# Cross-attention values as one-pass products of split context sums and split Wv

## What is computed

```python
q = rmsnorm((layernorm(x) @ Wq).reshape(B, Sq, H, D), gq)   # B=16, Sq=100, dim=512, H=16, D=128
k = rmsnorm((ctx @ Wk).reshape(B, Skv, H, D), gk)           # Skv=361, cdim=256
v = (ctx @ Wv).reshape(B, Skv, H, D)
attn = softmax(einsum('bqhd,bkhd->bhqk', q, k) / sqrt(D))
out = einsum('bhqk,bkhd->bqhd', attn, v).reshape(B, Sq, H * D)
x = x + out @ Wo
x = x + ffn(layernorm(x))      # rotations, 8-bit activations, ternary weights
```

## Time and profile before

| | |
|---|---|
| median of three runs | 1384.07 us (1384.0 to 1386.38) |
| the profiled execution | 1386.21 us, span 1384.4 us |
| TensorE products | 1361.0 us busy (98%) |
| VectorE | 949.7 us (69%) |
| ScalarE | 939.1 us (68%) |
| GpSimd | 442.0 us (32%) |
| granted TensorE clock, mean | 1.000 |

### The profile page before, as it was taken

The page is one execution under the profiler, slowest core; times in us unless marked ns, Lnnn a source line. Parts: engine busy times, 40 slices in busy tenths (PEclk is TensorE's granted clock), DMA queues, the critical chain, the costliest instruction groups (busy, mean ns, idle before and its releaser), DMA issues. The chain is left out here.

```text
span 1384.4 us, 28300 instructions
## 1 busy us (share of the span) xinstructions
PE 1361.0 (98%) x9496; PEld 1211.0 (87%) x9496; DVE 949.7 (69%) x2478; ACT 939.1 (68%) x2083; POOL 442.0 (32%) x349
## 2 busy tenths in 40 slices
PE   9999989999999999999999999999999999999997
PEld 9889867999999999999999999998878888888885
DVE  6312047668777877777778777776558778887886
ACT  5556668888888888888888888888734443444342
POOL 1034314322112212211222212213735555565551
PEclk9999999999999999999999999999999999999999
DMA  8867823333444444444434443435462342334212
GB/s 251 232 173 207 236 55 110 104 109 105 138 114 128 120 119 119 138 116 115 138 112 121 129 119 118 121 101 139 146 186 61 82 95 62 69 71 106 62 31 43
DMA packets 186403, 166.36 MB, mean 120 GB/s; under 512 B 87938, under 2 KB 155540, under 8 KB 184468
## 3 DMA queue, kind: packets, MB, share of 16 engines
q1 hardware_dynamic: 178980, 151.50, 39.6%
q10 hardware_dynamic: 7280, 13.06, 3.6%
HBM read 124.57 MB, written 33.02 MB: 114 GB/s over the span
## 5 line engine op out<-in xcount | busy, mean ns | idle before, releaser
L804 POOL TENSOR_TENSOR rk_sp<-ms_sp,neg_half 124x6 f32<-124x6 f32 x128 | 170.7, 1354 | 615.9 <-DMA ms_sp<-ms 615.9
L1028 ACT ACTIVATE pr<-ex,ri 100x361 f32<-100x361 f32 x256 | 153.6, 600 | 68.4 <-DVE ri L1228 68.4
L1240 DVE CUSTOM_DVE_ANT_0 sc<-psS,rk 100x361 f32<-100x361 f32 x256 | 136.3, 532 | 80.7 <-PE psS L879 65.7
L1021 ACT ACTIVATE ex<-sc,nb,rq_all 100x361 f32<-100x361 f32 x256 | 175.9, 687 | 2.2 <-DVE nb L1249 2.1
L907 PE MATMUL psZ<-pT_hi,cK_hi 120*128 120x400 f32 (+1 forms) x384 | 132.7, 346 | 0.0
L907 PE MATMUL psZ<-pT_hi,cK_lo 120*128 120x400 f32 (+1 forms) x384 | 132.2, 344 | 0.0
L907 PE MATMUL psZ<-pT_lo,cK_hi 120*128 120x400 f32 (+1 forms) x384 | 131.9, 344 | 0.0
L892 PEld LDWEIGHTS psP<-ident,pr 100*120 100x120 f32 (+1 forms) x768 | 73.0, 138 | 47.3 <-issue 35.3
L1228 DVE RECIPROCAL ri<-rs 100x1 f32<-100x1 f32 x256 | 41.3, 161 | 91.0 <-ACT ex L1021 87.0
L1220 DVE TENSOR_TENSOR pT_lo<-psP,pT_hi 122x600 fp32r<-122x600 f32 x128 | 99.0, 774 | 1.8 <-ACT pT_hi L1052 1.6
L922 PE MATMUL psNV<-z,wv_sb 128*128 128x200 f32 x504 | 97.2, 336 | 0.8 <-issue 0.8
(11 more groups left out here) (315 smaller groups left out, 3868.6 us busy)
## 6 DMA issues: line engine op xcount, KB each, us to landing
rk<-rk_dram SPq DMA_DIRECT2D x128, 290.6 KB
q_dram<-q_out SPq DMA_DIRECT2D x64, 200.0 KB, 4.6
q_in<-q_dram SPq DMA_DIRECT2D x64, 200.0 KB, 4.0
o_dram<-o SPq DMA_DIRECT2D x64, 200.0 KB, 4.5
stage<-in_w_ff SPq DMA_DIRECT2D x12, 1024.0 KB, 6.5
w_in<-in_w_ff ACTq DMA_DIRECT2D x48, 256.0 KB, 3.7
o_in<-o_dram SPq DMA_DIRECT2D x12, 1024.0 KB, 5.9
cT_in<-in_ctxT SPq DMA_DIRECT2D x15, 361.0 KB, 4.2
```

The source lines that it names most:

```text
L804: nc.gpsimd.tensor_tensor(rk_sp[:, cols], ms_sp[:, cols], neg_half[0:HG * SKR, :].to_broadcast([HG * SKR, n]), op=ALU.pow).then_inc(g_rk, 1)
L1021: nc.scalar.activation(ex[:, h % 2, :], sc[:, h % 2, :], ACT.Exp, bias=nb[:, h % 2:h % 2 + 1], scale=factor(n), accum_out=rs[:, h % 2:h % ...
L1028: nc.scalar.activation(pr[:, h, SKP - SK:SKP], ex[:, h % 2, :], ACT.Copy, scale=ri[:, h % 2:h % 2 + 1]).then_inc(a_pr, 1)
L1240: nc.vector.tensor_tensor_reduce(out=sc[:, h % 2, :], in0=psS[0:SQ, 0:SK], in1=rk[:, u % 2, h, 0:SK], scale=1.0, scalar=-3.0e38, op0=ALU.m ...
```

## The change

The values become three one-pass products per 128-row block: z_hi x wv_hi, z_hi x wv_lo, z_lo x wv_hi, so 12 products instead of 4 float32 ones (8 records) per value.

- Both halves of z are now split: ScalarE writes z_hi (`high_z`, at h=0 and h=2), VectorE z_lo (`low_z`, at h=0 and h=2, behind `negate_max`), both straight from psZ. z has two unit slots instead of four.
- Both values of a pair run in the odd unit: `values(u-3, psNV)` at h=2 and `values(u-2, psZ[1])` at h=3. `copy_o` of the second follows at h=0 of the next unit.
- GpSimd splits the pair's Wv columns (`split_wv`, eight operations of 2x128 columns at h=1 of even units) and the queries (`split_q`, two operations of 400 columns per unit, in place of ScalarE's `high_q` and VectorE's `low_q`). q_in has one slot instead of two, and `load_q` waits for the split of the unit before.
- To make room: seven slots for the squares instead of eight, the exponentials in place of the scores, `below` and `w_out` in one tile that also takes a block of Wo, xn0 and xr0 in w_in.
- One semaphore less in `queries`.

The core of the diff:

```diff
@@ attention: tiles
-        q_in = sb("q_in", [P, 2, UQ])
+        q_in = sb("q_in", [P, UQ])
-        sq = sb("sq2", [P, 2, HG, SKP])
+        sq = sb("sq2", [P, SQS, SKP])
-        ex, pr = sb("ex", [SQ, 2, SK]), sb("pr", [SQ, HG, SKP])
+        pr = sb("pr", [SQ, HG, SKP])
-        z = sb("z", [P, 4, CC, UQ])
+        z_hi, z_lo = sb("z_hi", [P, 2, CC, UQ], F32R), sb("z_lo", [P, 2, CC, UQ], F32R)
+        wv_hi, wv_lo = sb("wv_hi", [P, CC, HG * D], F32R), sb("wv_lo", [P, CC, HG * D], F32R)
@@ SP: load_q
-                if due(held(sp, u - 1)):
-                    sp.wait_ge(v_q, held(sp, u - 1))
+                if due(held(sp, u)):
+                    sp.wait_ge(g_qlo, held(sp, u))
@@ GpSimd
+            def split_q(u):
+                pool.wait_ge(d_q[u % 2], u // 2 * 16 + 16)
+                if due(u * HG - HG):
+                    pool.wait_ge(p_s, u * HG - HG)
+                nc.gpsimd.tensor_copy(q_hi[:, u % 2, :], q_in[:]).then_inc(g_qhi, 1)
+                pool.wait_ge(g_qhi, u + 1)
+                nc.gpsimd.tensor_tensor(q_lo[:, u % 2, :], q_in[:], q_hi[:, u % 2, :].bitcast(F32),
+                                        op=ALU.subtract).then_inc(g_qlo, 1)
+            def split_wv(p):
+                if due(p):
+                    pool.wait_ge(p_v, 2 * p)
+                for h in range(HG):
+                    col = (place(2 * p)[1] * HG + h) * D
+                    part = slice(h * D, (h + 1) * D)
+                    nc.gpsimd.tensor_copy(wv_hi[:, :, part], wv_sb[:, :, col:col + D]).then_inc(g_wv, 1)
+                    pool.wait_ge(g_wv, (p * HG + h) * 2 + 1)
+                    nc.gpsimd.tensor_tensor(wv_lo[:, :, part], wv_sb[:, :, col:col + D], wv_hi[:, :, part].bitcast(F32),
+                                            op=ALU.subtract).then_inc(g_wv, 1)
                     if h == 0 and real(u + 1, UNITS):
                         rms(u + 1, 1)
+                        split_q(u + 1)
+                    if h == 1 and u % 2 == 0 and real(u - 2, UNITS):
+                        split_wv((u - 2) // 2)
@@ TensorE: gather
-                    pe.wait_ge(v_z if c else a_z, u)
+                    pe.wait_ge(v_z, u * CC - CC + 1 + c)
+                if c == 1 and u % 2 == 0 and due(u):
+                    pe.wait_ge(a_o, u)
@@ TensorE: values
-                pe.wait_ge(a_z, first + 2)
-                pe.wait_ge(v_z, first + 2)
-                pe.wait_ge(v_ms, min(v + 6, UNITS))
+                pe.wait_ge(v_z, first * CC + 2 * CC)
+                pe.wait_ge(g_wv, (first // 2 * HG + v % 2 * 2 + 2) * 2)
+                if v % 2 == 0:
+                    pe.wait_ge(v_ms, min(v + 6, UNITS))
...
-                        last = nc.tensor.matmul(bank[:, k * 2 * SQ:(k + 1) * 2 * SQ], wv_sb[:, c, col:col + D],
-                                                z[:, first % 4:first % 4 + 2, c, h * SQ:(h + 1) * SQ],
-                                                start=(c == 0), stop=(c == CC - 1))
+                        for w, x in ((wv_hi, z_hi), (wv_lo, z_hi), (wv_hi, z_lo)):
+                            last = nc.tensor.matmul(bank[:, k * 2 * SQ:(k + 1) * 2 * SQ], w[:, c, h * D:(h + 1) * D],
+                                                    x[:, :, c, h * SQ:(h + 1) * SQ], start=(n == 0), stop=(n == 3 * CC - 1))
+                            n += 1
@@ TensorE: unit
-                    if h == 2 and real(u - 3, UNITS):
+                    if h == 2 and u % 2 == 1 and real(u - 3, UNITS):
                         values(u - 3, psNV)
-                    if h == 2 and u == UNITS + 1:
-                        values(UNITS - 1, psK[1])
                     if h == 3 and real(u - 1, UNITS):
                         gather(u - 1, 0)
+                    if h == 3 and u % 2 == 1 and real(u - 3, UNITS):
+                        values(u - 2, psZ[1])
@@ ScalarE
+            def high_z(u, c):
+                act.wait_ge(p_z, u * CC + 1 + c)
+                if due(u // 2 * 2):
+                    act.wait_ge(p_v, u // 2 * 2)
+                nc.scalar.activation(z_hi[:, u % 2, c, :], psZ[c][:, 0:UQ], ACT.Copy).then_inc(a_z, 1)
@@ VectorE
+            def low_z(u, c):
+                dve.wait_ge(a_z, u * CC + 1 + c)
+                nc.vector.tensor_tensor(z_lo[:, u % 2, c, :], psZ[c][:, 0:UQ], z_hi[:, u % 2, c, :].bitcast(F32),
+                                        ALU.subtract).then_inc(v_z, 1)
@@ VectorE: unit
-                    if h == 2 and real(u - 2, UNITS):
-                        copy_z(u - 2)
...
                         scale_scores(n, u, h)
                         negate_max(n, h)
+                    if h in (0, 2) and real(u - 2, UNITS):
+                        low_z(u - 2, h // 2)
```

More of the change, by code:

```diff
@@ L591, in attention @@
         bound = sb("bound", [P, 2])
-        w_in, below = sb("w_in", [P, 2, DIM]), sb("below", [P, DIM], BF16)
-        w_out = sb("w_out", [P, 2, DIM], FP8)
+        w_in, w_work = sb("w_in", [P, 2, DIM]), sb("w_work", [P, DIM])
+        below = w_work[:, 0:DIM // 2].bitcast(BF16)
+        w_out = w_work[:, DIM // 2:DIM].bitcast(FP8).rearrange("p (a n) -> p a n", a=2)
         psK = [bank0, ctx.enter_context(nc.psum_tensor("psK1", [P, 512], F32))]
@@ L613, in attention @@
                      cK_in[:].rearrange("p i c -> p (i c)")[:, 0:DIM]]
-                    + [sq[:].rearrange("p s h k -> p (s h k)")[:, i * DIM:(i + 1) * DIM] for i in range(5)])
+                    + [sq[:].rearrange("p s k -> p (s k)")[:, i * DIM:(i + 1) * DIM] for i in range(4)] + [w_work[:]])
         WO_HI_AT = {(UNITS - 3, 1): range(0, 4), **{(UNITS - 2, h): (4 + h,) for h in range(HG)}}
@@ L707, in spread_rk @@
                     sp.wait_ge(p_ss, UNITS)
+                    for i in range(2):
+                        sp.wait_ge(d_wt[i], 16 * CHUNKS // 2)
                     for i in range(4, 9):
@@ L866, in squares @@
                     rows = slice(h * QW32, (h + 1) * QW32)
-                    last = nc.tensor.matmul(psNV[rows, 0:SKP], sel[:, QW32 - 1:2 * QW32 - 1], sq[:, u % 2, h, :],
+                    last = nc.tensor.matmul(psNV[rows, 0:SKP], sel[:, QW32 - 1:2 * QW32 - 1], sq[:, (u * HG + h) % SQS, :],
                                             start=True, stop=True, tile_position=(0, h * QW32))
@@ L1097, in unit @@
                         high_cK(u // (2 * NG) * 2 + first - 1)
[L1098 to L1100 removed]
+                    if h == 3 and u % 2 == 1 and real(u - 3, UNITS):
                         copy_o(u - 3, psNV)
[L1102 to L1105 removed]
+                    if h == 0 and u % 2 == 0 and real(u - 3, UNITS):
+                        copy_o(u - 3, psZ[1])
+                    if h in (0, 2) and real(u - 2, UNITS):
+                        high_z(u - 2, h // 2)
                     if real(m, HEADS):
@@ L1287, in unit @@
                         low_cK(u // (2 * NG) * 2 + first - 1)
-                    if h == 2 and real(u + 1, UNITS):
-                        low_q(u + 1)
                     if h == 1 and real(u - 8, CHUNKS) and (u - 8) % NG == 0:
```

72 lines of the change are left out of this document (23 added, 49 removed).

## The result

The changed kernel takes 1418.26 us, the median of four runs (1417.62 to 1419.22), against 1384.17 us for the kernel before beside it (1384.0 to 1386.38): 1.0242 times as long, with an interval of 1.0229 to 1.0254. Its profiled execution took 1419.22 us, with a span of 1417.4 us against 1384.4.

A forecast was written before the change was run, and what follows sets the result against it. The prediction took TensorE's work to set the time of attention. Its terms, -2.2 + 8.3 + 7.4 + 2.4 + 1.9 = +17.8 us, gave 1402 us, with an own range of 1394 to 1411 and a wider one of 1383 to 1425.

The forecast's parts named there:

- Products, -2.2 us: TensorE's values: 12 products 112 ns apart take 1.344 against 1.378 us each, -2.2 us for 64 values.
- no one-pass product has under 256 columns: Reading of the earlier trace, given for the 98 ns rival: the load floor is shown only for f32 products.
- The odd unit's wait for z_lo, +8.3 us: Odd units, h=2: values wait for low_z behind scaling and negate_max, 0.26 us in each of 32 units.
- The even unit's wait for ring_lo, +7.4 us: After the shortened h=2 slot of even units, keys wait for low_k pushed back by low_z, 0.23 us in 32 units.
- GpSimd's lock, +2.4 us: Shared SBUF port: split_q meets VectorE's weight rounding, delaying TensorE 0.1 us in 24 even units.
- the removed high_q and low_q pay for the added high_z and low_z, four for four: ScalarE and VectorE: per pair, removed query splits were taken to offset the added context-sum splits.
- 1.4 us less time to catch up in this slot: Even unit's h=2 slot: ScalarE and VectorE lose this time; given with the upper bound of 0.5 us (16 us).
- The end, +1.9 us: End of attention: low_z behind first_norm and the residual's halves makes the first tile's transposes later; bounds 0 and 5.
- Products at 98 or 86 ns: Rivals on value product spacing: 98 ns, no load floor, 1391 us, chance 0.17; 86 ns, 1382 us, chance 0.15.
- many passes: Rival: short f32r products need as many passes as f32, 0.34 us each, +173 us, 1575 us; chance 0.07.
- Contention and lag: Rival: VectorE held for whole GpSimd subtractions (12 us) and even units late by 0.5 us (16 us), 1420 us; chance 0.15.

The follow-up runs named there:

- b_onepass: Kernel before with each value as 12 one-pass products of 200 columns, no low parts made, one value per unit as before; 1382.42 us, ratio 0.9987.
- a_prod: Kernel after with the products using z_lo last, TensorE waiting for z_hi before the first and z_lo before the fifth; 1405.92 us.
- b_late: Kernel before with VectorE's copy of half c=1 of the context sums moved behind scale_scores and negate_max, except in the last unit; 1395.92 us, ratio 1.0086.
- a_klo: Kernel after with VectorE's low_k ahead of low_z in every h=0 slot and in the h=2 slot of even units; 1411.16 us.
- a_wv_once: Kernel after with Wv split on GpSimd for the first pair only, all values reading that split; 1417.38 us.
- b_pair_late: Kernel before with both float32 values in the odd unit and VectorE's copy behind the scaling, nothing added on GpSimd; 1410.42 us, ratio 1.0188.
- b_pair: Kernel before with both float32 values of a pair in the odd unit, at h=2 and h=3, nothing split; 1391.03 us, ratio 1.0048.
- a_round_h3: Kernel after with the rounding of the feed-forward weights moved from the h=2 slot to the h=3 slot; 1416.33 us.
- a_best: Kernel after with the changes of a_klo and a_prod, and in the last unit low_z of half c=1 ahead of first_norm; 1396.06 us, ratio 1.0092.

## Why the prediction was right, and where it was off

The direction and the range held (1383 to 1425; 1418.3 measured), and so did the reasons given for the sign. The forecast of 1402 us was 16 us short: +17.8 us were summed up, +34 came. That the result lies in the range rests on a range of 42 us.

**Products, -2.2 us.** Right. The spacing is 0.111 to 0.112 us, and b_onepass gave -1.8 us. The floor of the earlier trace rows held for float32r. That the 128-column load sets it is only argued: transposes with 128-column loads (L316) are 0.086 us apart, and bfloat16 products of 128 columns in the feed-forward part (L1617) 0.056 us, so that "no one-pass product has under 256 columns" was misread, too. The Trainium skill, "TensorE: Matmul & The Clock Gate", section "LDWEIGHTS (loading the stationary operand)", would give an estimate of 107 ns for 128 columns and is 5 ns below the measured spacing. Its "Back-to-back issue gap" would give 86 ns for 200 columns as an isolated gap; these runs don't show that.

**The odd unit's wait for z_lo, +8.3 us.** The mechanism is right and a_prod shows it alone: 12.3 us, of which 11.5 in these slots. The term was mis-sized by about 0.1 us in each unit. z_lo came 0.71 us after the scaling's start (0.70 forecast) and TensorE followed as read from the earlier trace rows. But I let the scaling start 0.18 us after the scores, taking the queued copy out of the earlier trace rows. It starts 0.29 us after them in all 22 odd units. The copy had not held it: the row shows 0.18 us of idle time ahead of it. In the kernel before, too, the scaling in h=0 and h=2 never starts under 0.286 us behind the scores, in h=0 with VectorE idle for 0.6 us and no copy near, and in b_late, with the copy behind it, the least is 0.285. In h=1 and h=3 it is 0.175. So the changed kernel's own waits are not the reason either; why even and odd slots differ is open.

**The even unit's wait for ring_lo, +7.4 us, and GpSimd's lock, +2.4 us.** The place is right: 0.37 us in h3 of even units, 10.6 us over all units, against 9.8 forecast for both terms. a_klo removes all but 0.04 us of it by order alone, a_wv_once changes nothing of it, and b_pair_late has 0.34 us of it with no split on GpSimd. So the wait is the place of low_z ahead of low_k, as forecast, and not the lock. The lock came elsewhere. The rounding met a GpSimd split in 2 of its 48 units (32 and 38, 0.70 and 1.32 us instead of 0.48 and 0.75), not in 24, and the slots behind are 1.4 us longer in all; the split of cK in units 18 and 42 adds 0.5 us. At the start it costs more, 1.0 us in unit 1 and through the clock another 1.5, which the forecast did not hold.

**What was missed: odd h1, 0.37 us a pair, 8.8 us over all units.** The step that failed is "the removed high_q and low_q pay for the added high_z and low_z, four for four". The work is the same, and the busy times say so. But the query's parts stood at the end of a slot's list and no one waited for them. low_z of half c=0 stands in h=0 ahead of low_k, and waits for ScalarE, which in 12 units is 1 us late from the rounding in the short slot and has 0.8 to 1.0 us of cK or cT to split first. I worked out the slot h2 only and took the others as unchanged. b_pair adds that these units would be late even without it: the even unit's long h2 slot had been the reserve that covered their extra splits. That was named as a bound ("1.4 us less time to catch up in this slot") and not followed into the next unit.

**The end, +1.9 us.** The wait is right: 2.77 us idle against 0.84. The kernel paid 2.4 us more: 1.6 us from the start of the last two values on, where its clock fell to half, and 0.8 us ahead of the wait, which I did not follow up. The forecast held no fall of the clock, here or in units 1 and 61; its upper bound of 5 us was for another reason.

**The rivals.** Products at 98 or 86 ns and many passes are out by b_onepass. "Contention and lag", 1420 us, has the right size with half the wrong reason. It is lag in the main, of two kinds of which I priced one, and clock; contention has 1.9 us of the 21.7 in the steady stretch, and some more at the start.

## What to carry to other kernels

When work moves from one engine's slot to another, ask not only how long it is but what stands behind it in the same queue and what it waits for: an operation that needs a second engine, put ahead of one that doesn't, passes that engine's delays to everyone. A slot in which the bounding engine has extra work is a reserve for the others; emptying it brings out delays of units far from the change. Removing one of several stalls in a row may only show the next: a_klo took out 0.7 us a pair and 0.5 us came back one slot later, so read the slots one by one before believing a sum of gains.

## What the runs showed of the hardware

- One-pass float32r products of 200 columns with a full 128-column load each run 0.111 to 0.112 us apart, the same as 128-column and 3-column float32 ones, so the number of streamed columns does not set the pace there. The load before each is what the three have in common, but no run changes the load alone, and transposes with 128-column loads (L316) run 0.086 us apart.
- After TensorE had been idle for 2.77 us at the end of attention the granted clock fell from 1.00 to 0.50 (2.4 to 1.2 GHz) for some 3 us, with products running. In a_round_h3 it was at 0.50 for 6.8 us. But in a_klo, after the same 2.77 us, it stayed at 1.00, and so it did in a_wv_once. Shorter idle times can do it: it fell behind 2.14 us (unit 1 of the kernel after) and behind 0.89 and 0.78 us with six transposes between them (unit 61 of the kernel after, of a_wv_once and of a_klo), and in a_prod during a wait of 1.48 us that followed one of 0.59. Nor is the length of one idle time enough: in unit 2 it fell behind 1.96 us in a_klo and stayed at 1.00 behind 1.83 us in a_best. What decides it is open.
- VectorE's cK split of three operations took 1.83 us beside GpSimd's copy and subtraction of 128x256 tiles and 1.08 us beside GpSimd's powers of 124x6, while GpSimd's own copy took 0.59 us (0.40 is the median of the 128 copies in the kernel after). It took 2.11 us beside GpSimd's split of the queries (unit 1 of the kernel after) and 1.08 or 1.09 us in all 16 units of the kernel before. That agrees with the Trainium skill, "SBUF — State Buffer", section "SBUF: two separate sides", which calls the shared port pair an exclusive lock that one of the two engines holds for a whole instruction.
